# An attention and mixture-of-experts layer on one core: constant rows copied on the chip, two groups of small transposes each made one full product, and every engine's list written anew

## The chip, the core and the metric

The kernel runs on one core of one Trainium2 chip. A core has TensorE (PE in the profile: matrix products, with the loading of weights as PEld), VectorE (DVE), ScalarE (ACT), GpSimd (POOL) and SyncE (SP), which here does nothing but issue DMAs. The metric is the device time of one execution in microseconds, the median of three runs.

## What is computed

Sixteen sequences of 512 tokens with 128 features pass through one layer: a layer norm, causal attention with 16 heads of 64 features, a second norm with a gain and a shift inside the attention block, then a third norm and a mixture of 32 experts of which each token takes 8.

```python
x = x + attn(_layernorm(x))
x = x + ffn(_layernorm(x))

def attn(x):                                  # per sequence
    q, k, v = x @ Wq, x @ Wk, x @ Wv           # 16 heads x 64
    scores = where(causal, q @ k.T / 8, -inf)
    y = x + concat_heads(softmax(scores) @ v) @ Wo
    return (y - mean(y)) * rsqrt(var(y) + 1e-3) * gamma + beta

def ffn(x):
    probs = softmax(x @ gate_w.T)              # 32 experts
    top_w, top_idx = top_k(probs, 8)
    comb = one_hot(top_idx) weighted by top_w / sum(top_w)
    return sum over e of (u_e * silu(g_e)) @ down_e.T * comb[:, e]
```

All values are float32. The kernel splits each operand into two float16 parts (`_hi`, `_lo`) and makes each product out of three float16 products.

## The kernel before

The program has no loop on the chip and no scheduler. Each engine has a hand-written list of calls, such as `scores(n, 8, 0); times_v(n, 6, R1)`, and works through it in order; semaphores join the lists. A batch `m` is one sequence of 512 tokens, in four chunks of 128 (`C = 4`). The attention of batch n, the experts of batch n-1 or n-2 and the projections of batch n+1 are interleaved. The lists are written out for the batches 0 and 1, then once in a loop for n = 2 to 13, then written out for 14 and 15.

What the change touches:

- **Constant rows.** The score product of a head uses a stationary tile of 128 rows: 64 are the head's own, the other 64 carry constants (`KB0`, `KB1`, `KB2` on the side of the keys, `QB` on that of the queries). They bar the keys behind the query's position, and two of them (`MAX_ROWS`) carry the row maximum as a high and a low part. The tile `score_ops` keeps 5 slots x 2 heads of these, so each constant row stands there ten times. SP fills them at the start by four DMAs that read one row of HBM ten times over, lines 281 to 285. The first `scores` waits for them (`rows_loaded`, 80).
- **Loads at the start.** SP issues in this order: x of batch 0, identity, Wq, Wk, Wv, mask, gamma, beta, the constant rows, tail, Wo, gate_up, gate, down, and then x of batch 1. DVE takes the largest absolute value of each weight (`largest`, line 1043), from which ACT and DVE make the split weights `w_hi` and `w_lo` (line 789, line 1066).
- **Row maxima.** `max_scores` makes a rough product (64 rows of the array, `nat`), DVE reduces it to row maxima (line 1123), GpSimd scales and splits them for four heads at once (`split_maxima(m, g)`, g is one of 4 quads), PE turns them (`turn_maxima`, line 457: one transpose for each chunk, 8 columns of weights, four in a row), ACT copies the result (`copy_maxima`, 8 partitions x 512), and SP places it into `QB` by four DMAs (`place_max`, line 318). Only then can the first `scores` of the quad run.
- **Routing weights.** DVE makes `comb` (128 tokens x 4 chunks x 32 experts), PE turns it by four float32 transposes of 32 columns of weights (`turn_weights`, line 536), ACT copies 32 x 512, and SP stores it to HBM (`keep_weights`, line 324). `spread_weights` reads it back, each expert's row onto 64 partitions, and GpSimd multiplies (`weigh_unit`, line 1513).
- **GpSimd.** Its list has the norm's inverse deviations, `keep_h` (line 1482), `split_maxima`, `p_low` (line 1498, 256 of them: the low part of the softmax), `weigh_unit` and `unit_low`.

## Time and profile before

| | |
|---|---|
| median of 3 runs | 1783.02 us (1779.7 to 1785.89) |
| profiled execution: its own time | 1780.09 us |
| profiled execution: span | 1778.2 us |
| busy: PE | 1656.0 us (93%) |
| busy: DVE, ACT, POOL | 1454.3, 1421.6, 1380.2 us (82%, 80%, 78%) |
| granted clock of TensorE, mean | 0.99 |

The shares of busy time are means over stages with different limits. The core idles for a good part of its first 60 us; from about 200 to 1650 us PE is busy nearly all the time; after that the last batch drains. In the profile's rows a matmul's duration holds the time in which its result leaves the array, so the durations of matmuls that follow each other overlap. The distance from start to start is what a matmul takes of PE's time.

### The profile page before, as it was taken

The numbers are of one execution on the slowest core, as the hardware profiler recorded it, in microseconds if no ns is written. First come the engines' busy times: TensorE is split into PE (matmuls) and PEld (weight loads), VectorE is DVE, ScalarE is ACT, GpSimd is POOL, SyncE is SP. The second block draws the span as 40 slices with busy tenths as digits, with TensorE's granted clock in tenths as the row PEclk, the third lists the DMA queues.
The fourth block names the chain that finished last, engine by engine and source line by source line (L and its number), as shares of the span: only waits on it lengthen the run. The fifth ranks groups of instructions, "written<-read, shape, count | busy, mean of one in ns | idle before, by whom it ended". The sixth has DMA issues, their size and how long they took to land. (4 is left out here: it accounts for less than half of the span.)

```text
span 1778.2 us, 57403 instructions
## 1 busy us (share of the span) xinstructions
PE 1656.0 (93%) x21449; PEld 1122.7 (63%) x21449; DVE 1454.3 (82%) x4484; ACT 1421.6 (80%) x2364; POOL 1380.2 (78%) x1159
## 2 busy tenths in 40 slices
PE   1479999999999999999999999999999999999968
PEld 0146666676666666666666666667666666666645
DVE  2698887979888887979888897988889798787747
ACT  1279889889797978889798888979888897878842
POOL 0046689797988979787997988889797879879880
PEclk9899999999999999999999999999999999999999
DMA  7354553563555565364546445454544645544323
GB/s 192 84 124 100 125 132 100 156 151 92 152 126 141 118 163 133 106 154 122 139 120 158 126 119 152 117 144 120 151 122 124 155 110 148 132 131 112 105 84 103
DMA packets 216338, 228.61 MB, mean 129 GB/s; under 512 B 22674, under 2 KB 181630, under 8 KB 215806
## 3 DMA queue, kind: packets, MB, share of 16 engines
q1 hardware_dynamic: 216062, 224.94, 49.4%
q8 instruction: 172, 2.82, 0.7%
q14 instruction: 104, 0.85, 0.2%
HBM read 84.87 MB, written 5.24 MB: 51 GB/s over the span
## 5 line engine op out<-in xcount | busy, mean ns | idle before, releaser
L1498 POOL TENSOR_TENSOR p_lo<-p,p_hi 128x1280 f16<-128x1280 f32 x256 | 671.8, 2627 | 94.7 <-ACT p_hi L785 93.3
L847 ACT ACTIVATE p<-bank_s,back 128x512 f32<-128x512 f32 (+1 forms) x768 | 450.8, 614 | 37.2 <-PE bank_s L386 35.1
L386 PE MATMUL bank_s<-score_ops 128*128 128x62 f16 (+10 forms) x4096 | 402.6, 233 | 8.8 <-ACT p L847 7.5
L1513 POOL TENSOR_TENSOR expert_room<-expert_room 128x512 f32<-128x512 f32 x240 | 304.1, 1275 | 104.0 <-DMA expert_room<-comb_rows 100.8
L386 PEld LDWEIGHTS bank_s<-score_ops 128*128 128x128 f16 x4096 | 275.3, 97 | 170.1 <-ACT p L847 28.0
L785 ACT ACTIVATE p_hi<-p 128x1280 f16<-128x1280 f32 x256 | 324.4, 1267 | 5.3 <-PE bank_v L386 1.4
L1517 POOL TENSOR_TENSOR halves<-expert_room,halves 128x512 f16<-128x512 f32 x240 | 277.2, 1161 | 17.8 <-ACT halves L785 17.4
L1123 DVE CUSTOM_DVE_ANT_0 max_junk<-bank_r,mask 128x128 f16<-128x128 f32 (+3 forms) x519 | 228.7, 475 | 23.2 <-PE bank_r L386 8.6
L386 PE MATMUL bank_x<-w_hi,halves 128*128 128x128 f16 x1920 | 195.8, 219 | 3.1 <-POOL halves L1517 3.0
L785 ACT ACTIVATE halves<-expert_room 128x512 f16<-128x512 f32 x240 | 150.8, 629 | 46.2 <-PE bank_x L386 37.5
L386 PE MATMUL bank_x<-w_lo,halves 128*128 128x128 f16 x960 | 171.7, 219 | 0.0
L386 PEld LDWEIGHTS bank_x<-w_hi,halves 128*128 128x128 f16 x1920 | 154.3, 98 | 15.2 <-POOL halves L1517 4.5
L884 ACT ACTIVATE tanh_room<-bank_g,back 128x512 f32<-128x512 f32 x161 | 110.2, 685 | 44.7 <-PE bank_g L386 36.2
L1106 DVE TENSOR_TENSOR nat<-bank_r,nat 128x512 f16<-128x512 f32 x178 | 121.4, 682 | 24.4 <-ACT nat L785 24.2
L785 ACT ACTIVATE nat<-bank_r 128x512 f16<-128x512 f32 x178 | 104.5, 594 | 30.8 <-PE bank_r L386 21.7
L386 PE MATMUL bank_r<-hT,w_hi 128*128 128x512 f16 x356 | 107.7, 384 | 7.6 <-DVE hT L1101 4.5
L1218 DVE SCALAR_TENSOR_TENSOR expert_room<-tanh_room,bank_g 128x512 f32<-128x512 f32 x156 | 105.8, 678 | 10.7 <-ACT tanh_room L884 9.5
L1123 DVE CUSTOM_DVE_ANT_0 max_junk<-bank_u,mask 128x256 f16<-128x256 f32 (+3 forms) x204 | 103.5, 516 | 8.3 <-PE bank_r L386 5.5
L386 PE MATMUL bank_g<-tanh_room,w_hi 128*128 128x512 f16 x356 | 106.4, 380 | 0.1
L386 PE MATMUL bank_r<-tanh_room,w_hi 128*128 128x512 f16 x348 | 103.9, 380 | 0.8 <-DVE score_ops L1223 0.6
L386 PE MATMUL bank_r<-nat 64*128 64x128 f16 (+3 forms) x519 | 91.3, 300 | 14.1 <-DVE rowmax L1123 7.8
L386 PE MATMUL bank_v<-v_hi,p_hi 128*128 128x65 f16 x990 | 101.0, 195 | 0.1
(290 smaller groups left out, 4868.8 us busy)
## 6 DMA issues: line engine op xcount, KB each, us to landing
score_ops<-nat SPq DMA_DIRECT2D x256, 256.0 KB, 3.8
score_ops<-nat SPq DMA_DIRECT2D x512, 128.0 KB, 3.7
expert_room<-comb_rows SPq DMA_DIRECT2D x480, 128.0 KB, 3.0
xt<-in_x SPq DMA_DIRECT2D x16, 256.0 KB, 4.0
score_ops<-rowmaxT SPq DMA_DIRECT2D x256, 2.0 KB
xb<-in_x SPq DMA_DIRECT2D x16, 256.0 KB, 3.2
out_y<-expert_room SPq DMA_DIRECT2D x16, 256.0 KB, 3.8
score_ops<-comb_rows SPq DMA_DIRECT2D x32, 128.0 KB, 3.0
```

Of the source, the lines that this page charges most:

```text
L386: return pe.matmul(dst, lhsT, rhs, start=start, stop=stop, skip_group_check=shared)
L785: return act.activation(dst, src, ACT.Copy)
L847: act.activation(p32[:, h % P_SLOTS, at:at + cols], bank[score_bank(h, u)][:, 0:cols], ACT.Exp, scale=back[:, SC_SCORE:SC_SCORE + 1]).then ...
L884: act.activation(th, bank[b][:, :], ACT.Tanh, scale=back[:, SC_HALF:SC_HALF + 1]).then_inc(th_done, 1)
L1106: dve.tensor_tensor(nat[:, q % 2, (K_LO, Q_LO)[w], :], bank[b][:, :], nat[:, q % 2, (K_HI, Q_HI)[w], :], ALU.subtract).then_inc(proj_lo, 1)
L1123: done = dve.tensor_tensor_reduce(max_junk[:, k % 2, at:at + cols], bank[b][:, at:at + cols], mask[:, S - cols:S], 1.0, NEG, ALU.add, ALU. ...
L1218: dve.scalar_tensor_tensor(unit(p, j), th, 1.0, bank[b][:, :], ALU.add, ALU.mult).then_inc(gth_done, 1)
L1498: pool.tensor_tensor(p_lo[:, slot, :], p32[:, slot, :], p_hi[:, slot, :], ALU.subtract).then_inc(p_lo_done, 1)
L1513: pool.tensor_tensor(weighed(p, j), weighed(p, j), unit(p, j), ALU.mult).then_inc(a32_done, 1)
L1517: pool.tensor_tensor(a_lo[:, j % 2, :], weighed(p, j), a_hi[:, j % 2, :], ALU.subtract).then_inc(a_lo_done, 1)
```

## The change

Four things are done.

- Each of the four constant-row DMAs loads its row once, into the last slot. GpSimd then copies it to the other nine slots, 64 partitions x 4608 float16 each time, ahead of its first `split_maxima`. The first `scores` waits for the four copies too.
- `split_maxima` writes into a tile of 128 columns (`turnable`), of which 32 hold the maxima of four heads (4 heads x 4 chunks x 2 parts) and 96 are zero. `turn_maxima` becomes one product of this tile with the identity. `copy_maxima` copies 32 x 128, and `place_max` moves 8 partitions x 128 in each of its four DMAs, where it moved 2 x 512.
- `turn_weights` becomes one float32 transpose of 128 columns, `copy_weights` copies 128 x 128, and `keep_weights` stores by four DMAs where it used one.
- The lists of all five engines are written anew. The calls are the same; their order, and the PSUM bank that each takes, are not. One wait of `turn_h2` that another wait implies is left out.

```diff
-        rowmax = sb("rowmax", [P, QUADS, C, 4], F32)
-        rowmax_hl = sb("rowmax_hl", [P, QUADS, C, 2, 4], F16)
-        rowmaxT = sb("rowmaxT", [8, S], F16)
+        rowmax = sb("rowmax", [P, QUADS, 4, C], F32)
+        turnable = sb("turnable", [P, QUADS, P], F16)
+        rowmax_hl = turnable[:, :, 0:8 * C].rearrange("p g (k a h) -> p g k a h", k=2, a=2)
+        rowmaxT = sb("rowmaxT", [8 * C, P], F16)
...
-        combT, yT = late[0:NE, :], late[:, :].rearrange("p (c d) -> p c d", c=C)
+        combT, yT = late[:, 0:P], late[:, :].rearrange("p (c d) -> p c d", c=C)
...
             for n in range(3):
-                sp.dma_start(score_ops[E:P, 1 + n].rearrange("p a b s -> p (a b) s"),
-                             key_rows_c[:, n:n + 1, :].to_broadcast([E, 2 * SLOTS, S])).then_inc(rows_loaded, 16)
-            sp.dma_start(QB[E + MAX_ROWS:P].rearrange("p a b s -> p (a b) s"),
-                         query_rows_c.to_broadcast([BARS, 2 * SLOTS, S])).then_inc(rows_loaded, 16)
+                sp.dma_start(score_ops[E:P, 1 + n, SLOTS - 1, 1, :], key_rows_c[:, n, :]).then_inc(rows_loaded, 16)
+            sp.dma_start(QB[E:P, SLOTS - 1, 1, :], query_rows_c).then_inc(rows_loaded, 16)
...
                     for part in range(2):
-                        sp.dma_start(QB[E + part:E + part + 1, slot_of(m, 2 * g + k)].rearrange("a b s -> a (b s)").rearrange("a (b s) -> a b s", b=2),
-                                     rowmaxT[4 * part + 2 * k:4 * part + 2 * k + 2, :]).then_inc(max_placed[g], 16)
+                        at = 16 * k + 8 * part
+                        sp.dma_start(home[part:part + 1], rowmaxT[at:at + 8, :]).then_inc(max_placed[g], 16)
...
-                sp.dma_start(comb_rows, combT).then_inc(comb_stored, 16)
+                for c in range(C):
+                    sp.dma_start(comb_rows[:, c * P:c * P + P], combT[c * NE:c * NE + NE, :]).then_inc(comb_stored, 16)
...
-                for c in range(C):
-                    last = pe.transpose(half(b)[0:8, c * P:c * P + P],
-                                        rowmax_hl[:, g, c].rearrange("p a h -> p (a h)"), ident[:, :])
-                last.then_inc(rowmaxT_mm, 1)
+                mm(bank[b][:, 0:P], turnable[:, g, :], ident[:, :], True, True).then_inc(rowmaxT_mm, 1)
...
                 if m == 0 and h == 0 and u == 0:
                     pe.wait_ge(rows_loaded, 80)
+                    pe.wait_ge(rows_filled, 4)
...
-                for c in range(C):
-                    last = pe.transpose(bank[XB][0:NE, c * P:c * P + P], comb[:, c, :], ident32[:, :])
-                last.then_inc(combT_mm, 1)
+                pe.transpose(bank[XB][:, 0:P], comb[:, :, :].rearrange("p c e -> p (c e)"), ident32[:, :]).then_inc(combT_mm, 1)
...
-                copy(rowmaxT[:, :], half(b)[0:8, 0:S]).then_inc(rowmaxT_ready, 1)
+                copy(rowmaxT[:, :], bank[b][0:8 * C, 0:P]).then_inc(rowmaxT_ready, 1)
...
-                copy(combT, bank[XB][0:NE, :]).then_inc(combT_ready, 1)
+                copy(combT, bank[XB][:, 0:P]).then_inc(combT_ready, 1)
...
+            pool.memset(turnable[:, :, 8 * C:P], 0.0).then_inc(turnable_set, 1)
...
             inverse_deviation(0, 0, LN_EPS)
-            input_inverse(1); keep_h(0); split_maxima(0, 0); split_maxima(0, 1); p_low(0, 0); p_low(0, 1); p_low(0, 2)
+            pool.wait_ge(ln_shift[0], 1)
+            pool.wait_ge(rows_loaded, 80)
+            for side in (KB0, KB1, KB2, QB):
+                rows = side[E:P].rearrange("p a b s -> p (a b) s")
+                pool.tensor_copy(rows[:, 0:2 * SLOTS - 1, :], rows[:, 2 * SLOTS - 1:2 * SLOTS, :].to_broadcast([E, 2 * SLOTS - 1, S])).then_inc(rows_filled, 1)
+            pool.wait_ge(rows_filled, 4)
+            split_maxima(0, 0); keep_h(0); input_inverse(1); p_low(0, 0); split_maxima(0, 1); p_low(0, 1); p_low(0, 2)
```

How the change moves instructions is seen in the order of each engine. On SP, at the start of the program, before the change (a DMA's shape is partitions x rows x columns; `p_lo<-in_wo` is Wo, loaded into room that the softmax uses later):

```order
L280 DMA bet<-in_beta 128x128
L282 DMA score_ops<-in_key_rows 64x10x512 x3
L284 DMA score_ops<-in_query_rows 62x10x512
L286 DMA tail<-in_tail 128x132
L287 DMA p_lo<-in_wo 128x1024
```

and now:

```order
L283 DMA bet<-in_beta 128x128
L285 DMA score_ops<-in_key_rows 64x512 x3
L286 DMA score_ops<-in_query_rows 64x512
L287 DMA tail<-in_tail 128x132
L288 DMA p_lo<-in_wo 128x1024
```

The DMAs stand in the same order; the four of the rows have lost their factor of ten.

On POOL, after the first norm (`var_eps` to `shift` is one inverse deviation, `rowmax` to `rowmax_hl` one `split_maxima`), before:

```order
L1474 TENSOR_TENSOR shift<-minus_mean,rstd 128x4
L1468 TENSOR_SCALAR var_eps<-mv 128x4
L1469 TENSOR_SCALAR minus_mean<-mv 128x4
L1472 TENSOR_TENSOR rstd<-var_eps,minus_half 128x4
L1474 TENSOR_TENSOR shift<-minus_mean,rstd 128x4
L1482 COPY h_cur<-h 128x512
L1487 TENSOR_SCALAR rowmax<-rowmax 128x16
```

and now:

```order
L1472 TENSOR_TENSOR shift<-minus_mean,rstd 128x4
L1531 COPY score_ops<-score_ops 64x4608 x4
L1486 TENSOR_SCALAR rowmax<-rowmax 128x16
L1488 CAST turnable<-rowmax 128x2x8
L1490 TENSOR_TENSOR turnable<-rowmax,turnable 128x2x8
```

Four copies have come in between the first norm and the first `split_maxima`, and the second norm and `keep_h` have moved behind it.

On PE, in the middle of the loop, around a `turn_maxima` (a shape is rows of the result x columns streamed; `score_ops` are scores), before:

```order
L386 MATMUL bank_s<-score_ops 128x388
L386 MATMUL bank_s<-score_ops 128x62 x2
L457 MATMUL bank_v<-ident,rowmax_hl 8x128 x4
L386 MATMUL bank_s<-score_ops 128x384
L386 MATMUL bank_s<-score_ops 128x260
```

and now:

```order
L389 MATMUL bank_x<-w_lo,halves 128x128
L389 MATMUL bank_x<-w_hi,halves 128x128
L389 MATMUL bank_v<-ident,turnable 128x128
L389 MATMUL bank_u<-v_hi,p_hi 128x65
L389 MATMUL bank_u<-v_lo,p_hi 128x64
```

Four transposes that used 8 columns of the array are one product that uses all 128, as its neighbours do, and other work stands around it.

## Rows read from the trace of the kernel before

**Rows 1.** The page, part 1: busy time of each engine over the span.

```profile
PE 1656.0 (93%) x21449; PEld 1122.7 (63%) x21449; DVE 1454.3 (82%) x4484; ACT 1421.6 (80%) x2364; POOL 1380.2 (78%) x1159
```

**Rows 2.** Windows: stretch, length, busy us per engine, clock, DMA share, GB/s.

```profile
20.00:40.00 20.00, 0.00 (x0) 0.00 (x0) 0.00 (x0) 0.21 (x1) 0.00 (x0) 1.00 0.52 132
40.00:60.00 20.00, 2.10 (x9) 0.81 (x9) 7.82 (x24) 1.15 (x1) 2.22 (x5) 1.00 0.52 150
...
400.00:1600.00 1200.00, 1181.15 (x15598) 807.33 (x15596) 1021.71 (x3213) 1028.51 (x1721) 1022.64 (x856) 1.00 0.52 132
...
1700.00:1720.00 20.00, 17.52 (x237) 13.12 (x236) 10.68 (x20) 10.26 (x17) 20.00 (x16) 1.00 0.39 125
```

**Rows 3.** Timeline of the start: start us, duration us, instruction, idle before it.

```profile
9.53 21.19 SPq L286 DMA_DIRECT2D tail<-in_tail  x1
...
13.70 2.48 DVE L1066 SCALAR_TENSOR_TENSOR w_lo<-score_ops,w_scale,w_hi 128x1024 f16<-128x1024 f32 x2 [1.22 <-ACT w_hi L789]
...
16.70 1.21 DVE L1043 TENSOR_REDUCE w_absmax<-score_ops 128x1 f32<-128x1024 f32 x1
...
42.86 1.22 DVE L1043 TENSOR_REDUCE w_absmax<-p_lo 128x1 f32<-128x1024 f32 x1 [24.96 <-DMA p_lo<-in_wo]
...
54.86 0.87 DVE L1030 BATCH_NORM_STATS2 stats<-xt 128x6 f32<-128x128 f32 x4 [9.15 <-DMA xt<-in_x]
...
56.77 0.69 DVE L1123 CUSTOM_DVE_ANT_0 max_junk<-bank_u,mask 128x512 f16<-128x512 f32 x1
```

**Rows 4.** DMA view of 0 to 60 us, 40 slices of 1.5 us; issues with KB, us to landing.

```profile
GB/s 0 165 180 363 381 370 251 185 192 199 189 197 138 51 38 38 31 40 38 31 54 186 346 241 197 286 341 344 400 272 58 151 199 248 125 25 23 23 2 0
...
score_ops<-in_key_rows SPq DMA_DIRECT2D x3, 640.0 KB
```

**Rows 5.** GpSimd and VectorE: duration ns min/median/max, first and last start, form.

```profile
L1482 POOL COPY h_cur<-h x16: 600/612/624, 58.1 to 1556.5; 128x512 f32<-128x512 f32 x16
...
L1487 POOL TENSOR_SCALAR rowmax<-rowmax x64: 202/203/209, 75.3 to 1668.1; 128x16 f32<-128x16 f32 x64
...
L1498 POOL TENSOR_TENSOR p_lo<-p,p_hi 128x1280 f16<-128x1280 f32 x256 | 671.8, 2627 | 94.7 <-ACT p_hi L785 93.3
...
L1066 DVE SCALAR_TENSOR_TENSOR w_lo<-expert_room,w_scale,w_hi x4: 1278/2722/3369, 97.8 to 113.8; 128x1024 f16<-128x1024 f32 x4
L1066 DVE SCALAR_TENSOR_TENSOR w_lo<-score_ops,w_scale,w_hi x3: 1277/1280/1285, 13.7 to 63.1; 128x1024 f16<-128x1024 f32 x3
...
L1066 DVE SCALAR_TENSOR_TENSOR w_lo<-logits,w_scale,w_hi x1: 2195/2195/2195, 115.4 to 115.4; 128x32 f16<-128x32 f32 x1
```

**Rows 6.** Timeline of PE around one turning of maxima, in the loop.

```profile
711.58 0.39 PE L386 MATMUL bank_s<-score_ops 128*128 128x256 f16 x4
711.90 0.39 PE L457 MATMUL bank_v<-ident,rowmax_hl 128*8 128x128 f16 x4
712.22 0.39 PE L386 MATMUL bank_s<-score_ops 128*128 128x512 f16 x1
```

**Rows 7.** Timeline of PE around one turning of routing weights.

```profile
323.68 0.38 PE L386 MATMUL bank_r<-w_lo,hT 128*128 128x512 f16 x1
323.89 0.38 PE L386 MATMUL bank_r<-w_hi,hT 128*128 128x512 f16 x1
324.11 0.60 PE L536 MATMUL bank_x<-ident,comb 128*32 128x128 f32 x4
324.55 0.59 PE L386 MATMUL bank_g<-tanh_room,w_hi 128*128 128x512 f16 x2
```

**Rows 8.** Turned tiles: matmul, copies by ACT, store by SP, the longest waits.

```profile
L457 PE MATMUL bank_v<-ident,rowmax_hl x116: 219/219/220, 97.9 to 1646.9; 128*8 128x128 f16 x116
...
L785 ACT ACTIVATE rowmaxT<-bank_v x29: 570/587/587, 98.4 to 1647.1; 8x512 f16<-8x512 f16 x29
...
L324 SPq DMA_DIRECT2D comb_rows<-expert_room x16: 331/345/362, 209.2 to 1743.4; - x16
...
POOL expert_room L1513 <- DMA expert_room<-comb_rows: 100.8, 24, 8.6
```

More of the change, by code:

```diff
@@ new lines, in _ @@
+            scores(0, 0, 2); scores(0, 1, 0); scores(0, 1, 1); scores(0, 1, 2); max_scores(0, 3, 0, V, U)
+            max_scores(0, 3, 1, R0, R1); scores(0, 2, 0); max_scores(0, 3, 2, G, R0); scores(0, 2, 1)
+            max_scores(0, 4, 0, U, V); project(0, 10, R0); max_scores(0, 4, 1, U, R1); turn_maxima(0, 1, V)
+            scores(0, 2, 2); project(0, 11, G); scores(0, 3, 0); max_scores(0, 4, 2, V, U); times_v(0, 0, R0)
+            scores(0, 3, 1); project(0, 12, V); max_scores(0, 5, 0, U, G); scores(0, 3, 2); times_v(0, 1, R1)
@@ new lines, in _ @@
+            gate_product(13, 1, R0); max_scores(14, 7, 0, G, V); up_product(13, 0, R1); turn_weights(13)
+            scores(14, 10, 1); up_product(13, 1, G); gate_product(13, 2, U); project(15, 0, R0); project(15, 1, R1)
+            scores(14, 10, 2); up_product(13, 2, G); max_scores(14, 7, 1, U, R0); scores(14, 11, 0); times_v(14, 8, V)
+            times_v(14, 9, U); max_scores(14, 7, 2, G, R1); times_wo(14, 1, V); gate_product(13, 3, R0)
+            up_product(13, 3, U); values(15, 0, R1); gate_product(13, 4, G); values(15, 1, V)
@@ new lines, in _ @@
+            max_scores(15, 0, 0, R0, U); scores(14, 11, 1); down_product(13, 0); turn_maxima(14, 3, R1)
+            values(15, 2, R0); scores(14, 11, 2); up_product(13, 4, R1); gate_product(13, 5, V)
+            max_scores(15, 0, 1, U, G); up_product(13, 5, R0); turn_heads(14, 4, R1); project(15, 2, U)
+            down_product(13, 1); project(15, 3, V); values(15, 3, R1); scores(14, 12, 0); times_v(14, 10, R0)
+            gate_product(13, 6, G); max_scores(15, 0, 2, U, V); down_product(13, 2); scores(14, 12, 1)
@@ new lines, in _ @@
+            up_product(13, 7, R1); scores(14, 15, 0); turn_maxima(15, 0, U); times_v(14, 13, R0); scores(14, 15, 1)
+            up_product(13, 8, V); max_scores(15, 2, 1, R1, G); scores(14, 15, 2); gate_product(13, 9, U)
+            project(15, 6, V); down_product(13, 4); project(15, 7, G); max_scores(15, 2, 2, R0, R1)
+            turn_heads(14, 6, U); scores(15, 0, 0); scores(15, 0, 1); times_v(14, 14, R0); scores(15, 0, 2)
+            up_product(13, 9, V); down_product(13, 5); max_scores(15, 3, 0, U, R1); max_scores(15, 3, 1, V, R0)
@@ new lines, in _ @@
+            scores(15, 1, 0); scores(15, 1, 1); gate_product(13, 10, G); scores(15, 1, 2); times_v(14, 15, R1)
+            down_product(13, 6); max_scores(15, 3, 2, U, R0); turn_heads(14, 7, R1); gate_product(13, 11, V)
+            values(15, 4, R0); scores(15, 2, 0); project(15, 8, G); up_product(13, 10, R1); down_product(13, 7)
+            times_v(15, 0, U); scores(15, 2, 1); project(15, 9, R1); scores(15, 2, 2); turn_maxima(15, 1, G)
+            down_product(13, 8); up_product(13, 11, R0); max_scores(15, 4, 0, G, V); scores(15, 3, 0)
@@ new lines, in _ @@
+            project(15, 11, V); scores(15, 5, 2); down_product(13, 11); gate_product(13, 15, G); scores(15, 6, 0)
+            times_v(15, 3, U); max_scores(15, 5, 0, R0, R1); scores(15, 6, 1); project(15, 12, V)
+            max_scores(15, 5, 1, U, R0); times_v(15, 4, G); scores(15, 6, 2); scores(15, 7, 0)
+            max_scores(15, 5, 2, U, R0); down_product(13, 12); project(15, 13, U); up_product(13, 15, V)
+            project(15, 14, R1); scores(15, 7, 1); turn_maxima(15, 2, R0); down_product(13, 13); times_v(15, 5, G)
@@ new lines, in _ @@
+            logit_product(14); times_v(15, 8, U); times_wo(15, 0, V); gate_product(14, 0, R1); turn_weights(14)
+            scores(15, 10, 2); turn_heads(15, 3, G); scores(15, 11, 0); gate_product(14, 1, V); scores(15, 11, 1)
+            max_scores(15, 7, 2, R1, U); times_v(15, 9, R1); scores(15, 11, 2); up_product(14, 0, R0)
+            gate_product(14, 2, G); up_product(14, 1, R0); gate_product(14, 3, R1); turn_maxima(15, 3, V)
+            times_v(15, 10, R0); gate_product(14, 4, V); up_product(14, 2, U); times_wo(15, 1, G); up_product(14, 3, R1)
@@ L782, in _ @@
+            down_product(15, 13); down_product(15, 14); down_product(15, 15)
         @block.scalar
```

1156 lines of the change are left out of this document (562 added, 594 removed).

## The prediction, made before the changed kernel was run

> **What bounds the kernel now.** I read the page first, then windows, then the timeline of the parts where the windows show idle engines, then single lines. The page puts PE at 93% of the span, eleven points ahead of the next engine [rows 1], so 122 us of the span are not PE's. The windows say where they are: PE does nothing in 20 to 40 us and 2.1 us of work in 40 to 60, while in 400 to 1600 us it is busy 1181.15 of 1200 us [rows 2]. Near the end GpSimd, not PE, is full: 20.00 of 20 us in 1700 to 1720 [rows 2]. So there are three stages: a start in which nothing runs, a long middle bound by PE, and a tail bound by GpSimd and by the last batch's chain. PE's 98.4% in the middle is flattering, since durations include the draining of a result; I therefore read PE by the distance from start to start.
>
> The hole at the start has a visible cause. SP's issue of `tail` takes 21.19 us, from 9.53 on [rows 3]: the queue is full of the four row DMAs ahead of it, three of them 640 KB each [rows 4]. Together they are 2.5 MB, in packets of 1 KB. The rate shows them too: 363 to 381 GB/s while the first weights load, then near 190, then 31 to 54 GB/s in the slices from about 19.5 to 30 us [rows 4]. Wo can only be issued behind them, so DVE waits 24.96 us for it until 42.86. Then x of batch 1, behind 3 MB of expert weights, costs DVE another 9.15 us until 54.86 [rows 3]. DVE is a strict queue: everything behind these two waits is late by both.
>
> **The start.** The rows shrink to 4 x 64 KB. All loads up to Wo are then about 3.1 MB. At the 363 to 381 GB/s seen for weights [rows 4] they land by about 12 to 15 us. DVE is ready for Wo at 16.70 + 1.21 = 17.9 us [rows 3], so the wait of 24.96 us goes. gate_up (2 MB more) should land by about 21 us, before the new order wants it. The 9.15 us for x of batch 1 go as well: the new order takes x's statistics much later, behind the first maxima. Gain: 24.96 + 9.15 = 34.1 us.
>
> Against it stand GpSimd's copies. No copy of this size is in the trace. A copy of 512 elements takes 612 ns, a small operation on 16 elements 203 ns [rows 5]: (612 - 203) / 496 = 0.82 ns per element, hence 4.0 us for 4608 elements and 16 us for four. The bounds: an operation with two inputs takes 2627 / 1280 = 2.05 ns per element [rows 5], 9.5 us a copy; float16 at two elements in the time of one would make 2.1 us. I take 4.0, as a copy is nearest to a copy. They begin when the rows are in, near 14 us, and end near 30, or 34 with waits. The first `split_maxima` runs now at 75.3 us [rows 5]; moved ahead by 28 us it would come at 47. So the copies have about 13 us of cover on their own path. If a copy takes 9.5 us they end near 56 and the start loses 9 us more.
>
> They do have a side effect. Each `w_lo` of DVE reads two operands from SBUF. Alone it takes 1280 ns, but the four on `expert_room`, which run while GpSimd is at `p_low`, have a median of 2722 and a maximum of 3369; one over 32 columns took 2195 ns [rows 5]. A wait that doesn't shrink with the operand is a wait for GpSimd's current instruction to end. Three `w_lo` meet the copies: the first two, at 13.70 us [rows 3] directly ahead of the batch's first work, and that of Wv. Each can wait from 0 to 4.0 us, a whole copy; I take half, 6 us together. This agrees in kind with the Trainium skill (GPSIMD Engine Reference, Specifications): GpSimd shares SBUF interfaces with VectorE and contends with its instructions of two SBUF inputs. That rule speaks against putting copies here, but gives no price; mine is from the rows. Start: 34.1 - 6 = 28 us gained, from 19 (slow copies) to 34 (no meeting).
>
> **The products.** Four turned tiles of 8 columns take 0.39 us with 219 ns for one [rows 6, 8]: (390 - 219) / 3 = 57 ns from start to start. One product in place of four saves 3 x 57 = 171 ns. There is more around them. The scores at 711.58 stream 512 columns, which takes 0.21 us (323.68 to 323.89 [rows 7]), so the turning could start at 711.80; it starts at 711.90. It could end at 711.90 + 4 x 0.057 = 712.13; the next starts at 712.22 [rows 6]. So about 95 ns are lost on either side, though nothing is waited for. The same gap stands around the 64-row products of `max_scores`. A full product of 128 columns has no such gap. Counted in the program's order, the places where PE changes between full and partial tiles fall from 714 to 654: all 128 around `turn_maxima` go, but the new lists cut `max_scores` into more pieces and add back 68. In the loop it is 42 before and 40 now per batch, in batch 1 58 and 40, in batch 14 53 and 42.
>
> The Trainium skill (TensorEngine Tiling (Array Packing), Key Properties) says that a change of tiling mode drains TensorE. Taken by itself that would also give a gap around the routing weights, which use 32 columns: 2 x 95 x 16 = 3 us more. The rows show none: 323.89 + 0.22 = 324.11, and four turns from 324.11 to 324.55 are 4 x 110 ns with nothing behind [rows 7]. So I count only 3 x 110 = 330 ns for `turn_weights`.
>
> Per batch in the loop: 4 x 0.171 + 2 x 0.095 + 0.33 = 1.20 us, times 12 = 14.4. Batches 1 and 14: 2 x (0.684 + 0.33) + (18 + 11) x 0.095 = 4.8. Batches 0 and 15 lie in stages that PE doesn't bound; nothing. Together 19 us. Bounds: 14 if neither gap goes and only the streaming is saved, 22 if all sixteen batches pay.
>
> **The rest.** `copy_maxima` takes ACT 587 ns for 512 columns now [rows 8] and will take less for 128; ACT is not the bound, so nothing, but it shortens the way to `place_max`. Three more store DMAs per batch are 3 x 0.345 = 1.0 us of SP's queue [rows 8], with the spreading of weights and `place_qk` behind them. GpSimd waits for spread weights 24 times already, 100.8 us in all [rows 8], and has 1022.64 of 1200 us of work in the middle [rows 2]: hidden there. In the last batch it is on the path: +1.0, less 0.33 for PE and some 0.3 for ACT's shorter copy: +0.4 us.
>
> The lists. PE's visible idle time in the middle is 18.85 us per 1200 [rows 2], that is 1.6 us a batch. New lists cannot gain more than that, about 22 us over 14 batches, and can lose any amount. I see no side to lean to and take 0.
>
> Sum: 1780.1 (the profiled execution's own time) - 28 - 19 + 0.4 = 1733.5. The median of the runs lies 2.9 us above that execution; I say 1734.
>
> **Rivals.** (a) *The copies gate the first scores*, at 2.05 ns per element or because DVE and GpSimd block each other longer: 9 us and up to 6 more, 1743 to 1749. For it: the waits of `w_lo` in [rows 5]. Against: 13 us of cover. Chance 0.12. (b) *The new lists make PE wait.* If idle time in the middle doubles, +22 us: 1756. For it: the order was made for durations that nobody has yet measured. Against: neither ACT, DVE nor GpSimd is above 86% there. Chance 0.10. (c) *The rows were not what filled the queue*: the start stays, only the products are gained: 1761. Against: the issue that hangs directly behind them. Chance 0.03. (d) *Slower:* `place_max` lands late. Its DMAs carry the same bytes in 8 pieces of 256 bytes where there were 2 of 1 KB, and the first scores of each quad wait for them. With 64 quads the gain of 46 us and 5 us more are eaten once each waits 51 / 64 = 0.8 us. Against: between a turning and the scores of its quad the new lists keep, by the columns streamed, 4.9 us of products or more in the loop (5.6 before). At 1 us each it is 1798. Chance 0.03. (e) My forecast: 0.72.
>
> **The numbers.** The forecast's own range is 1716 to 1747: start 19 to 34, products 14 to 22, and at its low end 8 of the 22 us that lists could give. To leave out no more than 2 in 10 it must reach into (a) and the nearer part of (b): 1712 to 1752. Measurements of this kernel tell 0.3% (5 us) from no change. (a), (b), (c) and (e) are all faster: 0.96. Same 0.01, slower 0.03.
>
> **What the changed profile should show.** The issue of `tail` takes under 1 us, and DVE's reduction of Wo starts before 24 us with no wait above 3 us. Four copies of about 4 us each begin near 14 us. Some `w_lo` in that time takes 2 to 5 us. The first row maximum, now at 56.77 us [rows 3], comes near 29. A turning is one matmul with start to start of 55 to 60 ns and no gap beside full products. A batch in the loop takes about 1.2 us less. Wrong would make it: PE's idle time in the middle well off 1.6%, copies far from 4 us, or a tail that changes by more than 5 us.

## The result, and the profile after

The changed kernel takes 1749.67 us (median of 4 runs, 1747.59 to 1752.38), the kernel before 1784.15 us in the runs beside it (1779.7 to 1785.89). The ratio is 0.9821, 95% interval 0.9802 to 0.9841: about 32 us less. The forecast was 1734 us with a range of 1712 to 1752. The sign was right and the time lies near the upper end of the range; a third of the forecast gain did not come. The profiled execution took 1747.59 us, with a span of 1745.7 us.

The page of the changed kernel, part 1, against [rows 1]:

```profile
PE 1633.9 (94%) x21209; PEld 1113.7 (64%) x21209; DVE 1462.4 (84%) x4484; ACT 1404.4 (80%) x2364; POOL 1403.9 (80%) x1164
```

PE has 22 us less work and the span is 32.5 us shorter, so one could think that the products alone brought two thirds of it. The windows of the changed kernel, against [rows 2], say otherwise:

```profile
20.00:40.00 20.00, 9.47 (x27) 2.94 (x27) 18.17 (x29) 3.73 (x6) 11.17 (x3) 1.00 0.36 87
40.00:60.00 20.00, 12.60 (x58) 4.02 (x58) 19.33 (x54) 9.13 (x16) 1.18 (x4) 0.91 0.32 73
400.00:1600.00 1200.00, 1161.22 (x15302) 796.16 (x15300) 1012.20 (x3159) 1006.73 (x1694) 1020.52 (x844) 1.00 0.52 132
```

The empty 20 to 40 us are now busy, on VectorE above all (18.17 of 20). But in the middle PE is busy 1161.22 of 1200 us where it was busy 1181.15: its idle time went from 18.85 to 38.78 us, and it starts 296 instructions less in the same 1200 us (15302 for 15598), of which only some 175 are transposes that the change removes (15 a batch, 11.7 batches). The middle got slower (the length of a batch, below, settles it). The timeline of the start, against [rows 3]:

```profile
7.71 0.59 SPq L287 DMA_DIRECT2D tail<-in_tail  x1
...
13.24 17.93 POOL L1531 COPY score_ops<-score_ops 64x4608 f16<-64x4608 f16 x4 [6.26 <-DMA tail<-in_tail]
...
13.40 9.90 DVE L1067 SCALAR_TENSOR_TENSOR w_lo<-score_ops,w_scale,w_hi 128x1024 f16<-128x1024 f32 x2 [1.22 <-ACT w_hi L790]
...
24.95 1.20 DVE L1044 TENSOR_REDUCE w_absmax<-p_lo 128x1 f32<-128x1024 f32 x1
...
27.27 3.92 DVE L1052 TENSOR_SCALAR w_diagonal<-ident,w_peak 2x2 f32<-2x2 f32 x1
...
33.80 0.69 DVE L1124 CUSTOM_DVE_ANT_0 max_junk<-bank_v,mask 128x512 f16<-128x512 f32 x1 [1.12 <-PE bank_r L389]
...
35.63 1.27 DVE L1067 SCALAR_TENSOR_TENSOR w_lo<-score_ops,w_scale,w_hi 128x1024 f16<-128x1024 f32 x1
```

The issue of `tail` takes 0.59 us for 21.19, and the reduction of Wo waits for nothing; it starts at 24.95 us, where the forecast had it before 24. In their place VectorE spends 9.90 us on two `w_lo` (2.48 before) while GpSimd copies, and 3.92 us on a 2 x 2 scaling. Narrower windows of the same timeline show how the two engines take turns:

```profile
13.24 4.02 POOL L1531 COPY score_ops<-score_ops 64x4608 f16<-64x4608 f16 x1 [6.26 <-DMA tail<-in_tail]
13.40 4.94 DVE L1067 SCALAR_TENSOR_TENSOR w_lo<-score_ops,w_scale,w_hi 128x1024 f16<-128x1024 f32 x1 [1.22 <-ACT w_hi L790]
...
17.20 5.03 POOL L1531 COPY score_ops<-score_ops 64x4608 f16<-64x4608 f16 x1
18.26 5.04 DVE L1067 SCALAR_TENSOR_TENSOR w_lo<-score_ops,w_scale,w_hi 128x1024 f16<-128x1024 f32 x1
```

A copy with no `w_lo` running ahead of it takes 4.02 us. The first `w_lo` ends at 18.34, about 1.1 us after the first copy (17.26); the second copy lies behind that `w_lo` and takes 1.0 us more (5.03), and so on. So each `w_lo` waits for almost a whole copy. The first row maximum is at 33.80 (56.77 before).

For the length of a batch I take the first product on `tail`, once per batch in `scores(m, 0, 0)`, of batches 3 and 14. Before:

```profile
365.77 0.17 PE L386 MATMUL bank_s<-tail 128*128 128x4 f16 x1
...
1497.86 0.17 PE L386 MATMUL bank_s<-tail 128*128 128x4 f16 x1
```

and after:

```profile
323.53 0.17 PE L389 MATMUL bank_s<-tail 128*128 128x4 f16 x1
...
1470.42 0.17 PE L389 MATMUL bank_s<-tail 128*128 128x4 f16 x1
```

Eleven batches took 1132.09 us and now take 1146.89: 102.92 and 104.26 us each. Where the forecast had -1.2 us, there are +1.3. By the same product, the first scores of batch 0 start at 58.0 (92.2 before), 34.2 us earlier; batches 0, 1 and 2 take 73.5, 87.0 and 105.1 us (77.7, 94.6, 101.3), batch 14 101.4 (107.3), and from the first scores of batch 15 to the end are 173.9 (173.0). So: -34.2 at the start, -8.1 in batches 0 to 2, +14.8 in the loop, -5.9 in batch 14, +0.9 at the end, together -32.5.

### The profile page after: what moved, and what is told of

It is laid out like the page before. It is cut to its first block, busy times and chain, and to the rows that moved or that the text cites. A ratio compares the mean times of both kernels' runs of the same rounds, so it can differ in the third digit from the quotient of the medians.

```text
span 1745.7 us, 56980 instructions
## 1 busy us (share of the span) xinstructions
PE 1633.9 (94%) x21209; PEld 1113.7 (64%) x21209; DVE 1462.4 (84%) x4484; ACT 1404.4 (80%) x2364; POOL 1403.9 (80%) x1164
## 4 chain that ended last, share of the span: by engine, by line
PE 61%; SPq 8%; DVE 8%; DMA 6%; POOL 6%; issue 5%; ACT 5%; POOLq 0%; ACTq 0%; DVEq 0%
PE bank_r L389 15%; PE bank_s L389 12%; PE bank_v L389 8%; PE bank_g L389 8%; PE bank_u L389 8%; PE bank_x L389 7%; SPq L321 3%; POOL p_lo L1497 2%; DMA expert_room<-comb_rows 2%; SPq L335 2%; SPq L311 1%; SPq L312 1%; POOL expert_room L1512 1%; DMA xt<-in_x 1%; SPq L310 1%
## 5 line engine op out<-in xcount | busy, mean ns | idle before, releaser
L1512 POOL TENSOR_TENSOR expert_room<-expert_room 128x512 f32<-128x512 f32 x240 | 304.4, 1275 | 34.7 <-DMA expert_room<-comb_rows 17.4
L1124 DVE CUSTOM_DVE_ANT_0 max_junk<-bank_r,mask 128x384 f16<-128x384 f32 (+3 forms) x523 | 232.1, 474 | 36.6 <-PE bank_g L389 16.3
L389 PEld LDWEIGHTS bank_x<-w_hi,halves 128*128 128x128 f16 x1920 | 155.2, 98 | 20.3 <-issue 6.2
L389 PE MATMUL bank_r<-nat 64*128 64x384 f16 (+3 forms) x523 | 106.1, 300 | 15.3 <-DVE o L1137 9.8
L1124 DVE CUSTOM_DVE_ANT_0 max_junk<-bank_u,mask 128x512 f16<-128x512 f32 (+3 forms) x202 | 99.0, 505 | 6.1 <-PE bank_g L389 4.0
L389 PEld LDWEIGHTS bank_x<-w_lo,halves 128*128 128x128 f16 x960 | 94.1, 98 | 7.3
L389 PE MATMUL bank_r<-v_hi,p_hi 128*128 128x65 f16 x870 | 87.9, 194 | 2.1 <-POOL p_lo L1497 1.4
L389 PE MATMUL bank_r<-v_hi,p_lo 128*128 128x65 f16 x870 | 87.9, 194 | 0.0
L389 PE MATMUL bank_r<-v_lo,p_hi 128*128 128x64 f16 x870 | 87.8, 192 | 0.0
L786 ACT ACTIVATE nat<-bank_r 128x512 f16<-128x512 f32 x110 | 65.9, 599 | 26.2 <-PE bank_r L389 24.1
L389 PE MATMUL bank_u<-tanh_room,w_hi 128*128 128x512 f16 x264 | 78.7, 380 | 7.5 <-DVE v_lo L1112 6.2
L1124 DVE DVE_READ_ACCUMULATOR2_ANT rowmax<- 128x1 f32 x1024 | 85.2, 83 | 0.1
```

The source lines that it names most:

```text
L389: return pe.matmul(dst, lhsT, rhs, start=start, stop=stop, skip_group_check=shared)
L786: return act.activation(dst, src, ACT.Copy)
L1124: done = dve.tensor_tensor_reduce(max_junk[:, k % 2, at:at + cols], bank[b][:, at:at + cols], mask[:, S - cols:S], 1.0, NEG, ALU.add, ALU. ...
L1512: pool.tensor_tensor(weighed(p, j), weighed(p, j), unit(p, j), ALU.mult).then_inc(a32_done, 1)
```

## The experiments

Each kernel ran beside the kernel before on its chip. The ratios and their intervals are what to compare; 0.01 of the ratio is about 18 us.

| kernel | median us | ratio to before | 95% |
|---|---|---|---|
| changed kernel | 1749.67 | 0.9821 | 0.9802 to 0.9841 |
| rows_only | 1754.02 | 0.9850 | 0.9835 to 0.9865 |
| turned_only | 1789.90 | 1.0046 | 1.0031 to 1.0061 |
| all_old_lists | 1764.01 | 0.9904 | 0.9889 to 0.9919 |
| lists_only | 1772.34 | 0.9956 | 0.9942 to 0.9971 |
| max_only | 1770.55 | 0.9947 | 0.9929 to 0.9964 |
| weights_only | 1796.43 | 1.0086 | 1.0058 to 1.0114 |
| weights_one_store | 1785.13 | 1.0034 | 1.0020 to 1.0048 |
| old_lists_one_store | 1749.69 | 0.9835 | 0.9821 to 0.9850 |
| small_copies | 1750.27 | 0.9839 | 0.9810 to 0.9868 |
| max_first | 1732.75 | 0.9730 | 0.9700 to 0.9760 |
| max_first_scalar_copies | 1721.64 | 0.9674 | 0.9655 to 0.9693 |
| all_three | 1720.64 | 0.9673 | 0.9658 to 0.9687 |

**The change in parts.** The theory was the prediction's own sum (start, products, lists at nothing); the rival, that the lists or the new ways of moving data cost something. `rows_only` is the kernel before with the constant rows' lines of the diff alone:

```diff
-                sp.dma_start(score_ops[E:P, 1 + n].rearrange("p a b s -> p (a b) s"),
-                             key_rows_c[:, n:n + 1, :].to_broadcast([E, 2 * SLOTS, S])).then_inc(rows_loaded, 16)
+                sp.dma_start(score_ops[E:P, 1 + n, SLOTS - 1, 1, :], key_rows_c[:, n, :]).then_inc(rows_loaded, 16)
...
+                pool.tensor_copy(rows[:, 0:2 * SLOTS - 1, :], rows[:, 2 * SLOTS - 1:2 * SLOTS, :].to_broadcast([E, 2 * SLOTS - 1, S])).then_inc(rows_filled, 1)
```

> The kernel before with one edit: each constant row is loaded once and copied by GpSimd; old lists, old turnings. Theory A (the constant rows account for the start, and the middle lost because of the new order of the lists): two w_lo and one small VectorE operation wait for the copies as in the changed kernel (9.9 us for two w_lo, about 3.9 us for w_diagonal), the first row maximum stands near 34 us in place of 56.77, everything behind is earlier by about 23 us and the middle keeps its period: about 1757 us. Rival B (the whole 46 us that the changed kernel was ahead by its third batch come from the rows): about 1737 us. Rival C (the start is given back behind the first batch, since VectorE is full there): over 1770 us.

It measured a ratio of 0.985, 27 us less. Its first row maximum is at 32.89, its first scores at 67.2 us (25.0 earlier), and its PE does 1182.01 us of work in the middle (1181.15 before): nothing changed there (102.90 us a batch). This is the expectation's Theory A, and the start's term holds by itself.

`turned_only` has both turnings and the DMAs that go with them, in the old lists:

```diff
+                mm(bank[b][:, 0:P], turnable[:, g, :], ident[:, :], True, True).then_inc(rowmaxT_mm, 1)
...
+                        at = 16 * k + 8 * part
+                        sp.dma_start(home[part:part + 1], rowmaxT[at:at + 8, :]).then_inc(max_placed[g], 16)
...
+                pe.transpose(bank[XB][:, 0:P], comb[:, :, :].rearrange("p c e -> p (c e)"), ident32[:, :]).then_inc(combT_mm, 1)
...
+                for c in range(C):
+                    sp.dma_start(comb_rows[:, c * P:c * P + P], combT[c * NE:c * NE + NE, :]).then_inc(comb_stored, 16)
```

> The kernel before with the two turnings alone: the maxima of four heads by one product of 128 columns, the routing weights at once, with the placing DMAs of 8 pieces of 256 bytes and the four stores; old lists, old constant rows. Theory A (the turnings are worth what was counted, the lists lost it): 19 us less, about 1761 us, a period of about 101.7 us in the middle. Rival B (the finer DMAs land late or crowd SyncE's queue, and the waits of scores for placed maxima in the changed kernel come from them): the middle is no faster or slower than before, 1780 to 1800 us, with TensorE waiting for DMA score_ops<-rowmaxT.

It is slower than before, by 0.46%, though PE's busy time in the middle falls to 1159.89 of 1200 us, and a batch in the loop takes 103.80 us. The theory falls here: this part was to bring 19 us and costs 8. The time lies where Rival B had it, but not for its reason: PE's waits from 400 to 1600 us have no row for the placed maxima.

`all_old_lists` has every edit but the lists, `lists_only` the new lists alone (the diff's hunks of lists and the wait left out in `turn_h2`). One of the list lines, of SP:

```diff
-            load_x(1); place_qk(0, 0); place_qk(0, 1); load_x(2); place_qk(0, 2); place_max(0, 0); place_qk(0, 3)
+            place_qk(0, 0); load_xb(0); load_x(1); place_qk(0, 1); place_max(0, 0); place_qk(0, 2); place_qk(0, 3)
```

> All edits of the change, with the lists of the kernel before (GpSimd's list has the copies put in ahead). Theory A: the gains add, 23 us at the start and 19 us in the products: about 1738 us, 10 us faster than the changed kernel; a period near 101.7 us in the middle where the changed kernel has 104.3. Rival B (edits and lists belong together, since the old lists were made for other durations): 1747 us or more.

> The kernel before with the new lists alone: old constant rows, old turnings and DMAs. Theory A (the new lists make TensorE wait about 2.5 us more per batch in the middle, and gain at the start and in the last batches): their loss in the middle of about 29 us and their gain of about 20 us around it leave 1785 to 1795 us. Rival B (the waits in the middle come from the edits): the middle keeps a period of 102.9 us or less, and the total is 1765 us or less.

Measured were 0.9904 and 0.9956. The new lists gain with either set of edits: 8 us alone, and 0.9904 - 0.9821, some 15 us, with them. They gain at the ends and lose in the loop, as Theory A of the second text has it; the loss is smaller than its 2.5 us a batch, and the time lies between its 1785 and the rival's 1765. `all_old_lists` is 26 us slower than the sum of the gains in the first text, since one of the two gains didn't come, as `turned_only` shows. `lists_only` has its first scores 20.3 us earlier than the kernel before (71.8 for 92.2), batches 0 and 1 are shorter by 8.5 us together and batch 14 by 4.9, but batch 2 is 6.0 us longer and a batch in the loop takes 104.37 us, 1.45 more than before.

By the same product on `tail`, the length of a loop batch is

| | old lists | new lists |
|---|---|---|
| old products | 102.92 | 104.37 |
| new products, four stores | 103.80 (`turned_only`), 103.77 (`all_old_lists`) | 104.26 (changed kernel) |

With neither set of lists did the new products bring the 1.2 us a batch of the forecast: +0.9 in the old ones, -0.1 in the new ones. PE's idle time in the middle doubled in the old lists too (38.45 of 1200 us in `all_old_lists`, 38.78 in the changed kernel, 18.85 before).

**Which turning costs.** `max_only` takes the maxima's lines of the diff above, `weights_only` those of the routing weights.

> The kernel before with one edit alone: the maxima of four heads turned by one product and placed by DMAs of 8 pieces, lists, rows and routing weights as before. Theory C (the side cost of the turnings is that of place_max: the maxima arrive later at the scores, and all engines shift): about 1789, like both turnings together (1789.9). Theory D (it is the four stores of the weights in place of one, which hold GpSimd's spread weights back): about 1774, that is 1780.9 less some 7 us, as PE streams 0.7 us a batch less and nothing waits. Theory E (half from each): about 1782.

> The kernel before with one edit alone: the routing weights turned at once and stored by four DMAs, all else as before. Theory C: 1781 less 16 x 0.33 = 5 us, about 1776. Theory D: about 1788, with GpSimd's waits for comb_rows near 120 us in all, as in the run with both turnings, where they are 101 before. Theory E: about 1785.

The maxima gain 0.53%, the weights lose 0.86% (15 us). It is Theory D, and stronger than it said (1788 and 1774 expected, 1796 and 1771 measured). The way from the weights to GpSimd's first weighted unit shows why. Timeline of it in batch 5 before:

```profile
734.14 0.29 DVE L1209 TENSOR_TENSOR comb<-bank_x,exinv 128x128 f32<-128x128 f32 x1
...
735.98 0.35 SPq L324 DMA_DIRECT2D comb_rows<-expert_room  x1
...
738.14 3.70 SPq L332 DMA_DIRECT2D expert_room<-comb_rows  x6
...
741.73 3.82 POOL L1513 TENSOR_TENSOR expert_room<-expert_room 128x512 f32<-128x512 f32 x3 [7.76 <-DMA expert_room<-comb_rows]
```

and in `weights_only`:

```profile
741.88 0.29 DVE L1208 TENSOR_TENSOR comb<-bank_x,exinv 128x128 f32<-128x128 f32 x1
...
743.42 1.75 SPq L325 DMA_DIRECT2D comb_rows<-expert_room  x4
...
747.51 3.70 SPq L333 DMA_DIRECT2D expert_room<-comb_rows  x6
...
751.24 3.75 POOL L1512 TENSOR_TENSOR expert_room<-expert_room 128x512 f32<-128x512 f32 x3 [9.54 <-DMA expert_room<-comb_rows]
```

The shorter turning and copy bring the store forward by 0.3 us (1.54 us after `comb` for 1.84). But the first spread starts 4.09 us after the first store in place of 2.16, since it waits for the last of four. The whole way is 9.36 us for 7.59, and GpSimd stands still for it (9.54 us idle for 7.76).

In both kernels batch 5 is slower than most. The next one is closer to the rule. Before:

```profile
839.09 0.34 SPq L324 DMA_DIRECT2D comb_rows<-expert_room  x1
840.74 4.56 SPq L332 DMA_DIRECT2D expert_room<-comb_rows  x6
```

and in `weights_only`:

```profile
847.92 1.74 SPq L325 DMA_DIRECT2D comb_rows<-expert_room  x4
850.74 3.69 SPq L333 DMA_DIRECT2D expert_room<-comb_rows  x6
```

The medians over batches 3 to 13, read in the same way from the traces, are: from the store to the first spread 1.64 us before and 2.82 in `weights_only`, and for the whole way 7.08 and 8.16. So the way is 1.1 us longer in a usual batch. What is behind it on PE shows in PE's waits from 400 to 1600 us, before:

```profile
PE bank_r L386 <- DVE nat L1106: 4.0, 10, 1.3
...
PE bank_v L386 <- DVE expert_room L1223: 0.7, 2, 0.4
```

and in `weights_only`:

```profile
PE bank_v L387 <- DVE expert_room L1222: 6.9, 9, 1.1
...
PE bank_r L387 <- DVE nat L1105: 5.3, 14, 0.9
```

By these rows PE waited 0.7 us in all for VectorE's expert units and waits 6.9. The loop batch is 103.97 us (102.92 before): (1512.88 - 369.23) / 11. That is 1.05 us more, about what the way has grown by.

`max_only` has the other lesson. PE is busy for 1172.07 of the 1200 us of the middle, which is 100.2 us in a batch of 102.63 ((1489.55 - 360.60) / 11), where it was 101.3 us in one of 102.92. So PE's work falls by 1.1 us a batch (4 x 0.171 + 2 x 0.095 = 0.9 were forecast for the maxima), and the batch by 0.3 only. PE's waits for `nat` rose from 4.0 to 8.1 us and those for expert units from 0.7 to 3.4: it arrives earlier and waits for VectorE.

**One store in place of four.** The 128 rows of 512 bytes go out in one DMA:

```diff
-                for c in range(C):
-                    sp.dma_start(comb_rows[:, c * P:c * P + P], combT[c * NE:c * NE + NE, :]).then_inc(comb_stored, 16)
+                sp.dma_start(comb_rows.rearrange("e (c p) -> c e p", c=C), combT).then_inc(comb_stored, 16)
```

> The kernel before with the routing weights turned at once, but stored by one DMA of 128 rows of 512 bytes in place of four of 32 rows; lists, rows and maxima as before. Theory D2 (the way from the weights to GpSimd's first weighted unit sets the length of a loop batch in the old lists; it took 7.59 us before and 9.36 us with four stores, measured from VectorE's comb to GpSimd): the way is back at 7.3 us and the time is 1776 to 1781. Rival F (the turning itself, or where the copy of it lies, costs the time, and the count of stores doesn't): it stays at 1790 to 1796.

> All edits of the change except the new lists, with one store of the weights in place of four. Theory D2: the side cost is gone and the edits add up, 1754 (rows alone) less 11.6 (maxima alone) less up to 5 = 1737 to 1743. Rival F: no change from the same kernel with four stores, 1764.

With it the ratio goes from 1.0086 to 1.0034, and with all edits in the old lists from 0.9904 to 0.9835: the count of stores costs 9 to 12 us in these lists. But neither reached what Theory D2 said (1776 to 1781, 1737 to 1743). In batch 5 the way takes 7.6 us (`comb` at 737.3, GpSimd at 744.94), with the first spread 2.49 us after the store; PE still waits 3.4 us for expert units, and the loop batch is 103.22 us (102.68 with all edits in the old lists).

By batch 5 alone the way would be back at its old length, but the 7.59 us before was a slow one. By the medians of batches 3 to 13 the first spread starts 2.48 us after this store (1.64 before), and the way is 7.68 us, for 7.08 before and 8.16 with four stores. So the three kernels stand in the order of their ways: 0.6 us more way and 0.3 us more batch with one store of 512-byte rows, 1.1 and 1.05 with four. Theory D2 had the right link; its 7.3 us were not reached because this store, with short rows, is 0.8 us longer on its way to the first spread than the old one. Rival F is out as it was put, since the count of stores does cost time. `weights_one_store` still loses 6 us to the kernel before. The longer way points in that direction, but no run has the new turning with a way as short as before, so how much of the 6 us it explains stays open.

**The loop of the new lists.** Here PE waits for something else. Timeline of the changed kernel around the first scores of batch 7, SP's queue and PE:

```profile
734.39 0.61 SPq L310 DMA_DIRECT2D score_ops<-nat  x1
735.04 1.51 SPq L311 DMA_DIRECT2D score_ops<-nat  x1
736.60 0.61 SPq L312 DMA_DIRECT2D score_ops<-nat  x1
737.31 2.79 SPq L321 DMA_DIRECT2D score_ops<-rowmaxT  x4
...
741.31 0.38 PE L389 MATMUL bank_s<-score_ops 128*128 128x512 f16 x1 [1.92 <-DMA score_ops<-rowmaxT]
```

The turned maxima are copied by 733.21 us (ScalarE, 732.94 + 0.27), but `place_max(n + 1, 0)` stands behind `place_qk(n + 1, 2)` in SP's new list and starts at 737.31. The first scores, which want only pair 0, wait for it. It is the first row of PE's waits over the whole span:

```profile
PE bank_s L389 <- DMA score_ops<-rowmaxT: 15.3, 13, 2.2
```

(0.3 us in all before). `max_first` swaps the two calls in SP's loop:

```diff
-                spread_weights(n - 1, 9); place_qk(n + 1, 2); place_max(n + 1, 0); spread_weights(n - 1, 10)
+                spread_weights(n - 1, 9); place_max(n + 1, 0); place_qk(n + 1, 2); spread_weights(n - 1, 10)
```

> The changed kernel with place_max(n + 1, 0) put ahead of place_qk(n + 1, 2) in SP's list of the loop, nothing else. If the loop's first scores wait because the placing stands behind place_qk in that list, their 1.2 to 1.5 us a batch go: 1750 less 12 x 1.2 = 1735. If the wait only moves to the next late operand (the bank of max_scores(n, 6, 2), the low halves for up_product), less than a third of it is kept: 1746 or more.

It measured 0.973, 16 us better than the changed kernel by the ratios (17 by the medians), as expected if the order of the two calls is the cause. In `max_first` the wait is:

```profile
PE bank_s L389 <- DMA score_ops<-rowmaxT: 2.8, 5, 0.9
```

The batch is (1450.67 - 322.96) / 11 = 102.52 us, PE does 1174.97 us of work in 1200, and none of PE's other waits grew by more than 1 us. The loop gains 1.74 us a batch, 19 us in eleven; from the first scores of batch 15 to the end 4.0 us are given back (177.9 for 173.9); why stays open. What is left of PE's idle time in the middle is 25 us, 6 more than before, and its longest waits are for VectorE's `o` (8.1 us), `v_lo` (5.3) and `comb` (3.7), which are not among its waits of the kernel before.

**The copies.** `small_copies` cuts each of GpSimd's copies into nine:

```diff
-                pool.tensor_copy(rows[:, 0:2 * SLOTS - 1, :], rows[:, 2 * SLOTS - 1:2 * SLOTS, :].to_broadcast([E, 2 * SLOTS - 1, S])).then_inc(rows_filled, 1)
+                for n in range(2 * SLOTS - 1):
+                    pool.tensor_copy(rows[:, n:n + 1, :], rows[:, 2 * SLOTS - 1:2 * SLOTS, :]).then_inc(rows_filled, 1)
```

> The changed kernel with each of GpSimd's four copies of the rows cut into nine of one slot (512 elements, 0.5 to 0.6 us each), nothing else. If VectorE's low halves wait for the end of the GpSimd instruction that runs, the first two of 9.90 us fall to about 3 us each, the small scaling of the diagonal of 3.92 us to under 1 us, and the first row maximum comes some 8 us before 33.8: about 1742. If they wait for GpSimd to be idle, or for the port as such while bytes move, nothing is gained: 1749 to 1752.

Nothing was gained (0.9839), though the first half of it went as expected. Its timeline:

```profile
12.64 22.18 POOL L1532 COPY score_ops<-score_ops 64x512 f16<-64x512 f16 x36 [5.61 <-DMA tail<-in_tail]
...
13.16 3.27 DVE L1067 SCALAR_TENSOR_TENSOR w_lo<-score_ops,w_scale,w_hi 128x1024 f16<-128x1024 f32 x2 [1.22 <-ACT w_hi L790]
...
24.82 11.08 DVE L1067 SCALAR_TENSOR_TENSOR w_lo<-score_ops,w_scale,w_hi 128x1024 f16<-128x1024 f32 x1
```

The first two `w_lo` take 3.27 us (9.90 with whole copies), and the first row maximum came at 22.99. But the `w_lo` of Wv, which takes 1.28 us alone, then took 11.08 and ended at 35.90, 1.1 us after GpSimd's last copy (34.82). It sat through some sixteen copies of 0.6 us, not through the one that ran. Of the 10.8 us that the first row maximum gained, 9.8 were given back at this one instruction; the first scores came 0.9 us earlier (57.1 for 58.0).

`max_first_scalar_copies` is `max_first` with the copies taken from GpSimd and given to ScalarE, between its own first copies (`fill` is one copy):

```diff
+                act.activation(rows[:, 0:2 * SLOTS - 1, :], rows[:, 2 * SLOTS - 1:2 * SLOTS, :].to_broadcast([E, 2 * SLOTS - 1, S]), ACT.Copy).then_inc(rows_filled, 1)
...
+            h_high(0, G); fill(QB); qk_high(0, 0, R0); qk_high(0, 1, V); fill(KB0); qk_high(0, 2, U); halve_rest(2)
+            fill(KB1); v_high(0, 0, G); qk_high(0, 3, R0); v_high(0, 1, R1); fill(KB2)
```

> The changed kernel with place_max(n + 1, 0) ahead of place_qk(n + 1, 2), and with the four copies of the rows done by ScalarE, which sits idle from 14.9 to 25.5 us and from 27.3 to 33.3 us of the changed kernel, in place of GpSimd. If GpSimd's copies are what holds VectorE's low halves of weights at the start, the first two take 2.5 us and not 9.9, the third 1.3, the first row maximum comes near 23 us in place of 33.8, and the first scores come 8 us earlier: 1733 less 8 = 1725. If ScalarE's copies hold its own nat copies as long (4.8 us each), or if the first scores hang on something else, 1730 to 1738.

> The changed kernel with place_max earlier, the copies by ScalarE, and one store of the weights in place of four. Theory D2 with the new lists: GpSimd waits for comb_rows only 16.1 us in 15 times there, so the store is covered; 0 to 3 us better than without it, 1722 to 1725. If a store costs the same 1 us a batch in any lists: 1710.

Measured were 0.9674 and 0.9673, both 10 us better than `max_first` by the ratios, somewhat more than expected. In the timeline of `max_first_scalar_copies`:

```profile
13.47 2.48 DVE L1074 SCALAR_TENSOR_TENSOR w_lo<-score_ops,w_scale,w_hi 128x1024 f16<-128x1024 f32 x2 [1.22 <-ACT w_hi L795]
...
14.98 4.04 ACT L791 ACTIVATE score_ops<-score_ops 64x4608 f16<-64x4608 f16 x1
...
20.59 0.22 DVE L1059 TENSOR_SCALAR w_diagonal<-ident,w_peak 2x2 f32<-2x2 f32 x1
...
26.02 1.28 DVE L1074 SCALAR_TENSOR_TENSOR w_lo<-score_ops,w_scale,w_hi 128x1024 f16<-128x1024 f32 x1 [0.48 <-ACT w_hi L795]
```

Every one of the disputed instructions is at its time alone: 2.48, 0.22 and 1.28 us. The first scores start at 50.0 us, 7.6 earlier than in `max_first` (57.6). `all_three` adds the one store. It makes no difference that can be measured, where the same edit was worth 9 to 12 us in the old lists. GpSimd's waits for the spread weights are 17.4 us in all in the changed kernel and were 100.8 [rows 8], although the way itself is longer there (median 9.16 us): GpSimd has other work in it, and so the new lists give the store its cover. These two are the fastest kernels of the study, 26 us below the changed kernel by the ratios.

## Why the prediction was right or wrong

The direction was right, and so was the mechanism at the start. The mechanism in the middle was wrong: the step that failed is "a long middle bound by PE", by which work taken from PE was to shorten every batch in the loop by 1.2 us, with the stores at nothing. The runs showed +0.9 us with the same edits in the old lists (`turned_only`) and -0.1 in the new ones. By the ratios, the three terms were 28, 19 and 0 us and came out at 27 (`rows_only`), -8 (`turned_only`) and some 15 (the new lists, on top of the other edits). That the time still lay within the range is in part luck: the lists' gain stood in for the products'. The sum has a slip as well: it starts from the profiled execution (1780.1) and notes that the median lies 2.9 us above it, which makes 1736 and not 1734.

**The start** was forecast at 28 us from 19 to 34. `rows_only` gives 25 us at the first scores and 27 in all, so the cause, both waits and the size hold. The copies begin at 13.24 (14), and one with no `w_lo` ahead of it takes 4.02 us (4.0); the four take 17.93 us together because two of them wait for a `w_lo`. The cost of the meetings was mis-sized: half a copy for each of three `w_lo`, 6 us, was allowed. It was almost a whole copy for each of two, 9.90 - 2.48 = 7.4, plus 3.92 - 0.22 = 3.7 for a scaling that I had not counted, as it reads one tile; the third `w_lo` came after the copies and met none. 34.1 - 11.1 = 23.0, and that is what the first row maximum gained (56.77 to 33.80; the forecast had it at 29). The rule of the Trainium skill (GPSIMD Engine Reference, Specifications), that GpSimd contends with VectorE's instructions of two SBUF inputs, agrees with the two `w_lo`. The same row of that page names VectorE's instructions in a 2-port perf mode beside them. The scaling of a 2 x 2 piece, with one tile as input and a scalar from SBUF, was held as well, 3.92 us here and 0.22 with the copies on ScalarE; in which mode it ran no trace shows. The inference in the prediction, that a `w_lo` waits for the end of GpSimd's current instruction, fits the whole copies but not the small ones: there one `w_lo` sat through some sixteen.

**The products** were forecast at 19 us, from 14 to 22. This is the term that failed. Its pieces were right. One turning in the changed kernel:

```profile
732.62 0.22 PE L389 MATMUL bank_x<-w_hi,halves 128*128 128x128 f16 x1
732.68 0.22 PE L389 MATMUL bank_v<-ident,turnable 128*128 128x128 f16 x1
732.74 0.19 PE L389 MATMUL bank_u<-v_hi,p_hi 128*128 128x65 f16 x1
```

It takes 60 ns from start to start, with no gap on either side. The weights' turning takes 0.27 to 0.30 us where it took 0.60, and PE's busy time over the span fell by 22.1 us (1656.0 to 1633.9). What failed is the sentence that the middle is bound by PE, so that work saved there is time saved. At 98.4% busy PE still had 17 us of waits for others in 1200, and the batch did not follow it down: `max_only` kept 0.3 of 1.1 us. With the best list that I ran (`max_first`) the batch is 102.52 us, 0.4 less than before, where 1.2 were forecast. No run has that list without the new products, so what they are worth in it is not shown.

**The stores** were "hidden there", since GpSimd waits 100.8 us for spread weights already [rows 8]. That reading was upside down. An engine that waits 7.8 us in a batch for one chain has no cover to give to that chain: what is added to a link can be paid at once. The +1.0 us that I put into the last batch alone belonged to every batch in the old lists: 1.1 us more way in a usual batch, 1.05 us more batch.

**The lists** at 0: they gain 8 to 15 us, which is what is left of a gain at both ends after the loop, in which the batch of `lists_only` is 1.45 us longer than before. As a picture 0 was wrong, and as a sum it was off by up to 15 us. Rival (b), chance 0.10, describes the changed kernel's middle: PE's idle time doubled (18.85 to 38.78 us), and `max_first` puts 16 us of the time on one place in SP's new list. But the doubling alone doesn't single out the lists, since `all_old_lists` has it too, there with the four stores behind it. The rival's time was 1756; the lists' gain at the ends, 9 us of it in the start (34.2 us at the first scores for 25.0 in `rows_only`), is what made it less. Rival (d) had the right transfer, `place_max` late for the first scores of a quad, and the wrong reason and extent: not its pieces but its place in SP's list, and in one quad of four.

**Rival (a)** named a longer blocking of VectorE and GpSimd, and that part came: 11.1 us for 6, and with the copies on ScalarE 10 us come back. Its main part is out, the copies don't gate the first scores: these came 34 us earlier, and the copies ended 21 us before GpSimd's next work (its first `split_maxima` runs at 52.26). **Rival (c)** is out by `rows_only`. **The tail**: +0.4 forecast, +0.9 measured.

That `max_first` lands on 1733 us, where the forecast was, is chance: it has the new lists' gain at the ends in place of most of the products' gain in the loop.

## What to carry to other kernels

A wait of an engine is no cover for the chain that it waits for: before putting three more DMAs into a step, ask which engine waits for that step's end, and for how long in each round. When work is taken from the busiest engine, read what it waits for next (here 1.1 us of work saved a batch gave 0.3), and when lists are set anew, read the one operand that the first consumer wants and look where its transfer stands in the queue: two calls swapped were worth 16 us of 1750. Copies that nobody waits for are free only on an engine that doesn't hold another one: here that was ScalarE, not GpSimd.

## What the runs showed of the hardware that I had not expected

- A GpSimd copy held VectorE's instruction on a 2 x 2 piece for 3.92 us (0.22 alone), though it reads one tile and a scalar column.
- Cutting GpSimd's copies into pieces of 0.6 us did not bound VectorE's wait to one piece: one `w_lo` sat through about 11 us of consecutive copies. Two others in the same run took 3.27 us together. What decides which of the two happens was not found.
- The same copy, 64 partitions x 4608 float16, took 4.02 us on GpSimd when no `w_lo` was ahead of it, 5.03 when one was, and 4.04 on ScalarE, where VectorE's instructions beside it kept their times.
- One DMA of 128 rows of 512 bytes took 0.59 us to issue and 2.48 us from its issue to the next transfer that waits for it (medians of batches 3 to 13); one of 32 rows of 2 KB, with the same bytes, 0.34 and 1.64; four DMAs one behind another 1.74 and 2.82, and about 4.1 in three batches of eleven.
